# Four decay buffers, a ring of states of 10, a ring of loaded steps of 5 and a new step order in layer 1 of a two-layer kernel

## What is computed

```python
delta = softplus(dt_raw * W_dt[:, 0] + b_dt)          # per token and channel
def step(h, inp):                                     # over 512 tokens
    d_t, b_t, c_t, u_t = inp
    dA = exp(d_t[..., None] * A)                      # decay: 512 channels x 16 states
    h = dA * h + d_t[..., None] * b_t[:, None, :] * u_t[..., None]
    y = einsum('bds,bs->bd', h, c_t)
    return h, y
y = y + D_param * x_d
```

## Time and profile before

| | |
|---|---|
| runs | 1772.57 us median of 3 (1769.11 to 1778.48) |
| profiled execution | 1774.8 us, its span 1773.1 us |
| share of the span | PE 91%, DVE 83%, POOL 77%, ACT 76% |
| layer 1 | from about 557 us to the end |
| mean granted clock of PE | 0.969 of 2.4 GHz |

### The profile page before, as it was taken

One profiled execution on the slowest core, in us unless ns is written; L12 is line 12 of the kernel. 1 busy time (PEld: TensorE's weight loads), 2 busy tenths in 40 slices (PEclk: granted clock), 3 DMA queues, 4 the chain that ended last, 5 costly groups with the idle time before them and its releaser, 6 DMA issues.

```text
span 1773.1 us, 43498 instructions
## 1 busy us (share of the span) xinstructions
PE 1620.7 (91%) x13450; PEld 987.0 (56%) x13450; DVE 1477.5 (83%) x2750; ACT 1349.2 (76%) x3230; POOL 1367.5 (77%) x1114
## 2 busy tenths in 40 slices
PE   6788999999885888799999999999999999999988
PEld 3455687677563453465465456456556455545545
DVE  5787854356786989899989999999999999998996
ACT  5377877576663868878978978887887897797774
POOL 2059548862671188998999899899899999899995
PEclk9799999999988899999999999999999999999999
DMA  9633446596565743274373464445535446445430
GB/s 326 187 99 121 129 136 205 149 215 193 130 133 161 195 135 115 90 179 109 117 189 101 140 170 123 123 139 126 165 104 146 117 130 177 105 126 161 108 96 25
DMA packets 169963, 252.31 MB, mean 142 GB/s; under 512 B 31144, under 2 KB 114280, under 8 KB 169736
## 3 DMA queue, kind: packets, MB, share of 16 engines
q1 hardware_dynamic: 157448, 232.74, 46.5%
q0 software_dynamic: 12288, 16.79, 4.6%
HBM read 170.44 MB, written 75.86 MB: 139 GB/s over the span
## 4 chain that ended last, share of the span: by engine, by line
PE 37%; DVE 10%; issue 8%; ACT 7%; POOL 5%; DMA 1%; SPq 0%; DVEq 0%; ACTq 0%; POOLq 0%
PE bank L2382 32%; POOL HB L2333 3%; PE bank L2482 3%; DVE bank L2905 3%; DVE HB L2905 2%; ACT bank L2695 2%; POOL HB L2339 2%; DVE SU L2877 2%; ACT PR L2733 1%; DVE HB L2910 1%; ACT PT L2617 1%; PE bank L2510 1%; PE bank L2392 1%; DVE nmax L2936 0%; ACT PR L2726 0%
## 5 line engine op out<-in xcount | busy, mean ns | idle before, releaser
L2333 POOL TENSOR_TENSOR HB<-DD,BC 128x512 f32<-128x512 f32 x512 | 640.9, 1280 | 102.5 <-DMA DD<-SU 48.5
L2695 ACT ACTIVATE bank<-DD,A 128x512 f32<-128x512 f32 x512 | 349.4, 694 | 113.7 <-DVE HB L2910 72.4
L2339 POOL TENSOR_TENSOR HB<-HB,BC 128x512 f32<-128x512 f32 x256 | 324.4, 1284 | 30.7 <-DVE HB L2905 30.1
L2905 DVE TENSOR_TENSOR_SCAN bank<-bank,HB 128x512 f32<-128x512 f32 x256 | 310.8, 1214 | 21.9 <-ACT bank L2695 18.6
L2905 DVE TENSOR_TENSOR_SCAN HB<-bank,HB 128x512 f32<-128x512 f32 x256 | 310.0, 1211 | 10.3 <-ACT bank L2695 7.3
L2910 DVE TENSOR_TENSOR HB<-bank,BC 128x512 f32<-128x512 f32 x256 | 175.4, 685 | 15.9 <-DVE bank L2905 0.9
L2382 PE MATMUL bank<-HB,fold 128*32 128x512 f32 x1024 | 138.3, 612 | 20.5 <-DVE HB L2910 10.8
L743 POOL DMA_INDIRECT X<-expert_out_scratch,slot x64 | 108.0, 1687 | 40.6 <-issue 15.7
L2482 PEld LDWEIGHTS bank<-ident,PR 128*128 128x128 f32 x768 | 86.9, 142 | 82.9 <-issue 45.0
L2482 PE MATMUL bank<-ident,PR 128*128 128x128 f32 x768 | 114.6, 281 | 18.2 <-ACT PR L2733 8.7
L718 POOL TENSOR_SCALAR XSC<-XR,mv,scaled 128x256 f32<-128x256 f32 x64 | 94.2, 1476 | 41.1 <-DVE scaled L1383 36.4
(11 more groups left out here) (287 smaller groups left out, 3568.1 us busy)
## 6 DMA issues: line engine op xcount, KB each, us to landing
DD<-dd_scratch SPq DMA_DIRECT2D x488, 128.0 KB, 3.2
ROW<-row_scratch SPq DMA_DIRECT2D x64, 256.0 KB
BC<-ssm_scratch SPq DMA_DIRECT2D x128, 128.0 KB, 4.0
US<-us_scratch SPq DMA_DIRECT2D x32, 512.0 KB, 4.8
dd_scratch<-SU SPq DMA_DIRECT2D x16, 1024.0 KB, 6.0
us_scratch<-SU SPq DMA_DIRECT2D x15, 1024.0 KB, 6.5
XL<-sorted_scratch SPq DMA_DIRECT2D x78, 128.0 KB
expert_out_scratch<-YS SPq DMA_DIRECT2D x78, 128.0 KB
```

The costliest lines, as they stand in the source:

```text
L2333: done(pool.tensor_tensor(HB[:, c % HR], du, bc, ALU.mult), "dbu")
L2339: done(pool.tensor_tensor(h, h, bc, ALU.mult), "cg")
L2695: done(act.activation(PD[n % 2][:], delta, ACT.Exp, scale=A[:, k:k + 1]), "dA")
L2905: done(dve.tensor_tensor_scan(h if n % 2 else dA, dA, h, 0.0, ALU.mult, ALU.add), "scan")
```

## The change

The decay buffers become four: chunk n with n even uses PSUM bank 0 or 1, with n odd one of two SBUF tiles `PS`; ACT waits for chunk n-4. HB gets 10 slots, DD 5. To make room, `es` and `rows` lie in `SelT`. All numbers of `L1_ORDER` are new. The set of steps, the engine of each and the number of instructions stay the same.

```diff
-HR = 8
-DDS = 6
+HR = 10
+DDS = 5
...
-    "es": [[14]],
-    "rt": [[17, 18, 19, 20, 21, 32, 35, 39, 43, 47, 57, 66, 67, 69, 73, 81, 82, 83, 84, 85, 86, 87, 88, 89, 90, 105,
-        106, 107, 108, 111, 112, 113, 116, 135, 136, 137, 138, 139, 140, 141, 143, 167, 168, 169, 183, 190, 191,
...
+    "es": [[21]],
+    "rt": [[26, 29, 31, 35, 36, 39, 41, 45, 50, 54, 57, 61, 64, 67, 69, 71, 75, 77, 79, 81, 83, 84, 85, 86, 87, 88,
+        90, 91, 92, 93, 94, 95, 98, 101, 103, 105, 108, 110, 112, 113, 116, 119, 122, 124, 127, 128, 131, 132,
...
-    "del": [[115, 236], [674, 667], [1325, 1306], [1927, 1922], [2588, 2533], [3180, 3157], [3870, 3809], [4497,
+    "del": [[146, 164], [704, 694], [1306, 1274], [1954, 1910], [2570, 2538], [3186, 3178], [3869, 3812], [4500,
...
-    "kr": [[205]],
-    "keys": [[220]],
+    "kr": [[138]],
+    "keys": [[142]],
...
-        es, rows, part = sb("es", [T]), sb("rows", [T]), sb("part", [2])
+        es, rows, part = SelT[:, 0], SelT[:, 1], sb("part", [2])
...
-        PD, PY = PB[0:2], PB[2]
+        PS, PY = sb("PS", [2, T]), PB[2]
...
+        def decays(n):
+
+            return PS[:, n // 2 % 2] if n % 2 else PB[n // 2 % 2][:]
...
                 def decay(b, n):
                     delta = dd_loaded(act, b, n)[:, 0]
-                    if b == 0 and n < 2:
+                    if b == 0 and n < 4:
                         after(act, "asc", 0, 0)
-                    if n >= 2 or b:
-                        after(act, "scan" if n % 2 else "mult", *chunk(NCH * b + n - 2))
+                    if n >= 4 or b:
+                        after(act, "scan" if n % 2 else "mult", *chunk(NCH * b + n - 4))
                     k = 4 * (4 * (n // 16) + n % 4) + n // 4 % 4
-                    done(act.activation(PD[n % 2][:], delta, ACT.Exp, scale=A[:, k:k + 1]), "dA")
+                    done(act.activation(decays(n), delta, ACT.Exp, scale=A[:, k:k + 1]), "dA")
...
                 def scan(b, n):
                     after(dve, "dA", b, n)
                     after(dve, "dbu", b, n)
-                    dA, h = PD[n % 2][:], HB[:, (NCH * b + n) % HR]
+                    dA, h = decays(n), HB[:, (NCH * b + n) % HR]
                     done(dve.tensor_tensor_scan(h if n % 2 else dA, dA, h, 0.0, ALU.mult, ALU.add), "scan")
...
-                    done(dve.tensor_tensor(HB[:, (NCH * b + n) % HR], PD[n % 2][:], bc, ALU.mult), "mult")
+                    done(dve.tensor_tensor(HB[:, (NCH * b + n) % HR], decays(n), bc, ALU.mult), "mult")
```

More of the change, by code:

```diff
@@ new lines @@
+    "conv": [[56, 60, 62, 66, 68, 70, 74, 76, 78, 44, 47, 51], [448, 455, 461, 472, 481, 485, 463, 470, 478, 497,
[5 rows of a table added]
+    "gam": [[42, 37, 49, 109, 55, 99]],
+    "x_ld": [[22], [964], [1607], [2190], [2880], [3500], [4153], [4768]],
+    "xrt": [[20, 23], [542, 530], [1241, 1234], [1882, 1887], [2506, 2477], [3152, 3154], [3759, 3796], [4400,
+        4422]],
+    "xrtc": [[28, 30], [545, 533], [1302, 1300], [1892, 1919], [2562, 2606], [3188, 3190], [3846, 3829], [4414,
+        4498]],
+    "silu": [[73, 89, 82, 63], [518], [1115], [1752], [2393], [3031], [3663], [4296]],
@@ new lines @@
+    "us_st": [[97, 117], [534], [1128], [1770], [2408], [3048], [3679], [4312]],
+    "dtb": [[100]],
+    "gsilu": [[111]],
+    "proj": [[162, 157, 120, 150, 134, 130, 126, 166, 80, 65, 72, 172, 288, 304, 339, 312, 348, 381, 354, 362, 524,
[10 rows of a table added]
+    "abs": [[121, 118, 144, 133], [606, 597, 610, 604], [1202, 1207, 1212, 1209], [1840, 1846, 1843, 1850], [2489,
+        2483, 2486, 2493], [3128, 3117, 3131, 3123], [3749, 3748, 3743, 3753], [4441, 4406, 4419, 4446]],
+    "sexp": [[129, 156], [652], [1244], [1879], [2522], [3135], [3776], [4452]],
@@ new lines @@
+    "sln": [[136, 160], [686], [1262], [1898], [2531], [3168], [3784], [4481]],
+    "relu": [[143, 115, 140, 149], [613, 641, 616, 628], [1298, 1222, 1204, 1218], [1946, 1831, 1834, 1837], [2559,
+        2518, 2496, 2500], [3164, 3155, 3126, 3119], [3859, 3844, 3755, 3805], [4386, 4391, 4388, 4383]],
+    "del": [[146, 164], [704, 694], [1306, 1274], [1954, 1910], [2570, 2538], [3186, 3178], [3869, 3812], [4500,
+        4489]],
+    "asc": [[32]],
+    "du": [[154, 173], [725, 716], [1329, 1295], [1971, 1928], [2589, 2555], [3250, 3216], [3889, 3827], [4521,
+        4512]],
@@ new lines @@
+    "pad_st": [[19]],
+    "turn": [[198, 208, 238, 242, 277, 271, 369, 323, 440, 464, 509, 538, 567, 572, 595, 598, 640, 629, 675, 664,
[39 rows of a table added]
+    "scan": [[182, 204, 197, 186, 231, 246, 226, 269, 298, 281, 305, 317, 336, 322, 340, 332, 356, 352, 365, 375,
[28 rows of a table added]
+    "turnc": [[207, 216, 247, 250, 284, 276, 374, 334, 449, 469, 513, 571, 574, 578, 624, 639, 646, 633, 682, 667,
[10 rows of a table added]
+    "mult": [[194, None, 211, None, 243, None, 256, None, 310, None, 328, None, 346, None, 349, None, 370, None,
[28 rows of a table added]
+    "rec": [[209, 241, 280, 309, 599, 740], [828, 885, 991, 1130, 1282, 1400], [1480, 1530, 1581, 1675, 1914, 2037],
+        [2126, 2154, 2225, 2323, 2578, 2660], [2753, 2802, 2852, 2974, 3204, 3287], [3380, 3484, 3535, 3600, 3833,
+        3922], [4021, 4065, 4142, 4224, 4467, 4557], [4661, 4707, 4747, 4849, 5007, 5098]],
@@ new lines @@
+    "keys": [[142]],
+    "value": [[220, 261, 409, 498, 565, 581, 585, 655, 659, 691, 796, 803], [990, 998, 1098, 1154, 1236, 1243, 1267,
[34 rows of a table added]
+    "fold": [[224, 283, 343, 376, 421, 431, 486, 517, 559, 590, 618, 647, 724, 769, 779, 835], [892, 907, 962, 1001,
[7 rows of a table added]
+    "kst": [[145]],
+    "w_ld": [[181], [706], [1286], [1924], [2551], [3187], [3822], [4501]],
+    "spreadc": [[222, 308, 330, 423, 676, 754], [857, 1020, 1108, 1192, 1311, 1450], [1500, 1661, 1693, 1820, 1965,
+        2060], [2220, 2242, 2288, 2461, 2594, 2670], [2789, 2931, 2948, 3046, 3223, 3299], [3443, 3547, 3610, 3708,
+        3854, 3936], [4110, 4221, 4241, 4338, 4487, 4591], [4678, 4806, 4866, 4901, 5020, 5108]],
@@ new lines @@
+    "ranks": [[303], [749], [1410], [2025], [2671], [3292], [3911], [4575]],
+    "dd_st": [[200], [735], [1342], [1982], [2602], [3263], [3901], [4531]],
+    "sel": [[318, 315, 307, 311], [765, 762, 758, 755], [1452, 1441, 1490, 1463], [2062, 2057, 2077, 2065], [2686,
+        2678, 2752, 2709], [3313, 3308, 3303, 3301], [3929, 3920, 3926, 3917], [4587, 4744, 4620, 4579]],
+    "xg": [[326], [782], [1542], [2184], [2765], [3354], [4034], [4761]],
+    "xgc": [[342], [800], [1559], [2210], [2783], [3373], [4053], [4774]],
@@ new lines @@
+    "h_load": [[], [347], [799], [1558], [2208], [2782], [3371], [4052]],
+    "st": [[406, 402], [941, 937], [1595, 1591], [2475, 2359], [2865, 2898], [3477, 3478], [4130, 4132], [4780,
+        4781]],
+    "stv": [[408], [942], [1599], [2364], [2903], [3494], [4141], [4786]],
+    "skip": [[407, 525, 677, 853], [1007, 1126, 1264, 1461], [1627, 1757, 1907, 2088], [2265, 2402, 2529, 2725],
+        [2888, 3032, 3166, 3350], [3522, 3661, 3794, 3990], [4155, 4310, 4458, 4629], [4763, 4921, 5063, 5150]],
@@ new lines @@
+    "exp": [[None, None, None, None, None, None, None, None, 398, 387, 503, 487, 551, 569, 587, 593, 636, 622, 671,
[10 rows of a table added]
+    "gate": [[414, 528, 683, 861], [1013, 1135, 1293, 1465], [1631, 1761, 1911, 2097], [2268, 2415, 2544, 2775],
+        [2894, 3042, 3173, 3388], [3533, 3677, 3799, 3996], [4162, 4314, 4464, 4642], [4769, 4924, 5074, 5151]],
+    "dt_ld": [[], [579], [1183], [1814], [2464], [3095], [3728], [4366]],
+    "sta": [[411], [951], [1601], [2480], [2872], [3482], [4151], [4785]],
+    "widenr": [[695, 842], [1334, 1477], [1987, 2119], [2617, 2748], [3245, 3394], [3885, 4040], [4522, 4676],
+        [5038, 5125]],
@@ new lines @@
+    "tail": [[900, 868, 925, 879], [1504, 1486, 1573, 1518], [2123, 2136, 2150, 2160], [2795, 2821, 2841, 2855],
+        [3447, 3414, 3405, 3463], [4116, 4089, 4050, 4064], [4746, 4727, 4704, 4687], [5158, 5155, 5152, 5153]],
+    "tailc": [[908, 883, 944, 894], [1568, 1523, 1590, 1531], [2139, 2152, 2161, 2174], [2817, 2842, 2857, 2866],
+        [3470, 3428, 3415, 3481], [4137, 4103, 4078, 4094], [4757, 4751, 4719, 4717], [5161, 5159, 5154, 5156]],
+    "out": [[911, 887, 948, 899], [1571, 1527, 1594, 1535], [2149, 2156, 2164, 2178], [2826, 2846, 2860, 2870],
+        [3475, 3432, 3418, 3486], [4140, 4107, 4092, 4102], [4760, 4753, 4722, 4720], [5163, 5162, 5157, 5160]],
```

148 lines of the change are left out of this document (43 added, 105 removed), and 504 rows, old and new, of the table L1_ORDER.

## The result

| | before | after |
|---|---|---|
| median of 4 runs | 1774.44 us (1769.11 to 1778.48) | 1949.9 us (1947.23 to 1952.39) |
| profiled execution, its span | 1774.8 us, 1773.1 us | 1947.23 us, 1945.5 us |
| first POOL product of layer 1 | 609.4 us | 620.4 us |
| the same, counted from DVE's first step of layer 1 | 51.8 us | 66.9 us |
| from the first product to the end of the span | 1163.7 us | 1325.1 us |

The change makes the kernel 1.0991 times as long, with a 95% interval of 1.0956 to 1.1025. The forecast was 2024 us, in a range from 1945 to 2125.

A forecast was written before the change was run, and what follows sets the result against it. PE was taken to bound layer 1 before, POOL after. First product 619.4, POOL's work 1054.35, odd scans 307, idle 30 and end 13.5 made a 2024.3 us span; forecast 2024 us, range 1945 to 2125.

The forecast's parts named there:

- the price of an odd scan: Layer 1: each of 256 odd scans with two SBUF inputs costs POOL 1.2 us, 307 us in all.
- The second rival: Layer 1: DVE's odd scans wait for POOL's products, +0.89 us each, so DVE bounds; 1954 us, chance 0.08.
- the first case: Layer 1: odd scans block POOL's SBUF reading and POOL becomes the bound; 2024 us, chance 0.80.
- the part behind the last product: End of the kernel: 13.5 us from POOL's last product to the end of the span.
- the gaps of POOL as a reserve: Layer 1: POOL's 95.9 us of idle time would take 80 of the 256 odd scans.
- it gains: Rival: scans leave POOL its reads and deeper rings close PE's gaps, if a scan costs under 0.37 us; 1752 us, chance 0.06.
- 30 us of idle POOL time: Layer 1 after the change: of POOL's 95.9 us idle, 30 us stay; bounds 0 and 95.9.
- PE bounds: Layer 1 before the change: PE, busy 1088.9 of 1150.2 us, sets the time, POOL 11 us per batch behind.
- Decays four deep: Layer 1: ACT runs four chunks ahead, its 107.7 us of waiting mostly go, but this brings nothing.
- Ring of 10: Layer 1's ring of states: POOL waits less for fold, part of its 95.9 us idle time saved.
- Ring of 5: Layer 1's ring of loaded steps: costed at 0, or up to 9.5 us once or twice.
- The order: Start of layer 1: more routing rounds and key steps before DVE's first step addition, +10 us; bounds 0 and +14.

The follow-up runs named there:

- s1: Kernel before, with its order, rings and two decay buffers, only the odd buffer moved from PSUM to SBUF; 1948.36 us, ratio 1.0961.
- all2: Kernel before with both of its two decay buffers moved to SBUF; 2293.12 us in a single run.
- h64: Kernel before with only every eighth chunk's decay (64 of 512 scans) in SBUF, the others in PSUM; ratio 1.0298.
- xd: Kernel before plus an idle DVE reduction with one SBUF input ahead of each of the 256 odd scans; ratio 1.0612.
- xp: Kernel before plus an idle 256-column POOL product ahead of each of the 256 odd drive products; ratio 1.0539.
- s2: Kernel before, old order and rings, with the change's four decay buffers and ACT four chunks ahead; 1948.74 us, ratio 1.0962.
- b_half: Kernel before with POOL's products of odd states with C done on 256 of 512 columns; 1772.42 us, ratio 0.9979.
- r2: Kernel before with a ring of states of 10, decays in PSUM, old order; 1774.91 us, ratio 1.0004.
- a1: Changed kernel with batch 0's first step addition and product earlier on DVE and key stores behind the first step loads; 1944.5 us, ratio 1.0971.

## Why the prediction was right or wrong

**Right: what does it.** Two SBUF inputs in the odd scans make POOL's products and DVE's scan exclude each other. s1 has this without the new order and rings and takes 1948 us, the change 1950; all2 scales it up; the even scans, untouched, keep their 1.21 us. The time is another matter: 175 us were lost where 250 were forecast, and 1950 lies 5 us above the lower end of the range. It lies inside only because the range was drawn down to the rival in which DVE waits, and that rival did not come true as it was told.

**Wrong: the price of an odd scan, 1.2 us for POOL.** This is the term of the sum that failed. The hold of one scan is 1.01 us by the estimate above (2287 - 1275 ns), below even the lower bound of 1.15, which was scaled from the 1.37 of 1.44 us of layer 0's scan. And not every scan holds a product for all of it: POOL's busy time in the stretch rose by 191.6 us, 0.75 per scan, where 307 us were forecast (-115). The other part of the waiting fell on DVE, whose busy time rose by 139.9 us. The sum assumed that POOL bears all of it, since the scans of the earlier trace rows and the tensor_tensor of the earlier trace rows had lost nothing; they showed only one half of the exchange, the one in which POOL waits.

**The second rival was half true.** The scans did wait, +0.64 us each against 0.89 in the rival's one row (613.25). Its number, 1954 us, lies nearer to 1950 than the forecast, but not its reason: DVE is busy for 1207 us, not 1295, and POOL is the fuller engine. The true case is both at once, and the prediction had split it into two that exclude each other. Its test "products grow, or scans grow" had no place for what came. The signs named for the first case came out short: a mean product of 1.49 us for 1.7, held ones of 2.29 us at most for 2.4 to 2.7, POOL at 94.7% of the stretch for 97.

**The other terms.** Idle time of POOL was taken at 30 us and is 70.2 (+40); the part behind the last product at 13.5 and is 9.0 (-4.5); POOL's first product at 619.4 and is at 620.4 (+1). With -115 these make 1945.5 out of 2024.3, to a rounding. The +1 is luck: the new order costs 15.1 us at the start, not 10, and layer 0 happened to end 4 us earlier in the profiled execution of after.

**Wrong: the gaps of POOL as a reserve.** The prediction had the 96 us of gaps swallow the first 80 scans and drew the threshold of "it gains" from them (0.37 us per scan). h64 costs 53 us by the times and 59 by the stretch, where by that step it is nearly free. xd and xp show the same without held scans: of the 142 us laid on DVE 76% come out at the end, of the 143 on POOL 70%. With 256 scans at 0.75 us the old step would give 191.6 - 95.9 = 96 us plus the start, too little: the stretch grew by 161.4. POOL's idle time took only 25.7 us of the 191.6, and the shorter end 4.5.

**Wrong in the sum as well: 30 us of idle POOL time.** The gaps were taken to close to 30 us because POOL would bound. From its first to its last product POOL stands idle for 69.4 us in s1, 69.6 in s2 and 70.2 in after: the odd scans in SBUF bring it down from 95.9, and neither the depth nor order and rings move it further. In after 42.6 us of it are waits for odd scans and 22.3 for folds. What would close them is not shown.

**"PE bounds" was incomplete.** PE was busy for 1089 of 1150 us, so 96 us of room was read for POOL and 83 for DVE. Lightening POOL brings at most 0.4% (b_half), as was expected of an engine that does not bound; loading it by 143 us costs 99 (xp). Both are true together. In the stretch after, PE's share fell to 86.6%, not to 80, and its mean granted clock from 0.99 to 0.95 while the idle time between its matmuls rose; its busy time rose by 51 us, with 1% more matmuls in the records.

**Decays four deep: right at 0, on a wrong ground.** ACT's waits were to mostly go; they are 107.1 + 75.2 us in after. In the old order they do go, 233 to 28 us from s1 to s2, and nothing is gained. In s2 at least, ACT's waits set nothing.

**Ring of 10.** Forecast as some part of POOL's 96 us; alone it brings 0 (r2), as the wait moves from fold to the scans. **Ring of 5:** right at 0 as far as it can be seen: POOL waits 1.3 us in all for such a load in after and ACT 12.0, and the loads land in 2.9 us at the median and 5.5 at most. By itself the ring of 5 was not tried.

**The order.** Together with the rings it gains some 17 us in the stretch (after against s2) and loses about 15 at the start, so that nothing is left of it in the time. The loss at the start has the reason that the prediction gave: the rounds and key steps ahead of line 2971 bring the first addition 14.5 us later, and a1, which takes half of that back, takes back 6.9 us of the first product. Its size was forecast too small (+10, at most +14, measured +15.1): 13.3 + 1.3 = 14.6 us of rounds and key steps came out in full, and DVE's pause of 4.64 us gave nothing back: it shrank to 2.42, but a new one of 2.38 came up ahead of a small step (line 2872), and up to the first addition DVE is idle for 9 us before and 10 after. The prediction found "nearly the same sequence" in SP's queue; there the key stores had moved ahead of the first loads of steps, for which a1 shows no cost.

**Left open.** The new order with all decays in PSUM was not tried: it is made for four buffers, and there are not two more banks. Whether its 17 us would be there without the held products is not known. The old order with a ring of 5 was not tried either. Which of the new order's places, or the ring of 10, brings the 17 us in the stretch is not known. No version that does the whole computation beats the kernel before.

## What to carry to other kernels

While POOL reads SBUF most of the time, keep one input of each frequent two-input instruction of DVE in PSUM: here the move of one of two buffers cost 10%, and a gain of depth around it could not be seen. When two engines exclude each other, price the loss on both, from rows in which each has been the one to wait. In an order that is written out, do not count the idle time of a second engine as full reserve: before a term is set against gaps, put idle work of that size there, and see what comes out at the end. And when two executions are compared by the place of one instruction, count from a step that moves with what lies ahead: here 4 us of another layer stood in for 4 us of a wrong forecast.
